# A new order for the last stage of a two-layer network: scores two tiles ahead, the last mix between the upper products, the router shortened

## What is computed

```python
A = softmax((X @ W_q + b_q) @ (X @ W_k + b_k).T / 16); x = layernorm(x + A @ (X @ W_v + b_v))
scores = sigmoid(xf @ gate.T); sfc = scores + corr_bias       # 8 experts in 2 groups of 4
group_scores = top_k(sfc.reshape(N, 2, 4), 2)[0].sum(-1)      # two best of each group
# keep the better group, take its two best experts, normalise their scores
lat = xf @ fc1_w.T
he = relu(lat @ w1[e].T) ** 2 @ w2[e].T                       # for each expert e, weighted and summed
shared = relu(xf @ up_w.T) ** 2 @ down_w.T
x = layernorm(x + comb @ fc2_w.T + shared)
```

## Time and profile before

| | |
|---|---|
| median of three runs | 2061.44 us (2057.5 to 2069.4) |
| the profiled execution | 2061.02 us, of it span 2059.3 us |
| mean granted PE clock over the span | 0.958 of full speed |
| busy over the span | PE 91%, DVE 69%, ACT 42%, POOL 36% |
| one batch of stage C, third of eight | 156.32 us, PE busy 147.09 us |

### The profile page before, as it was taken

How to read it: one execution, slowest core, us unless ns; L and a number is a source line. 1 busy time by engine, 2 the same in 40 slices (tenths; PEclk the granted TensorE clock), 3 DMA queues, 4 the chain that set the end, 5 groups by cost and what they waited for, 6 DMA issues and landing times.

```text
span 2059.3 us, 35698 instructions
## 1 busy us (share of the span) xinstructions
PE 1873.7 (91%) x11728; PEld 1640.9 (80%) x11728; DVE 1413.4 (69%) x3599; ACT 873.6 (42%) x1623; POOL 749.9 (36%) x774
## 2 busy tenths in 40 slices
PE   7999998469999986999999999999999989999997
PEld 6888887359999975878878878878878878878876
DVE  3788787644444446786886886886787787787666
ACT  3445454332322334345445445445445435444433
POOL 4145555431122014244245245145145145144033
PEclk8999999679999997999999999999999999999999
DMA  3111121032222232112112112112112112111011
GB/s 108 62 62 62 62 82 62 22 123 82 92 90 90 81 122 74 32 42 83 42 42 83 37 47 83 37 47 84 34 50 83 32 53 83 32 52 52 11 42 62
DMA packets 80860, 129.94 MB, mean 63 GB/s; under 512 B 11184, under 2 KB 62000, under 8 KB 80720
## 3 DMA queue, kind: packets, MB, share of 16 engines
q1 hardware_dynamic: 71840, 103.91, 15.0%
q0 software_dynamic: 8880, 24.26, 5.0%
HBM read 103.48 MB, written 24.67 MB: 62 GB/s over the span
## 4 chain that ended last, share of the span: by engine, by line
PE 31%; DVE 17%; issue 7%; ACT 4%; POOL 2%; DVEq 0%; DMA 0%; ACTq 0%; POOLq 0%; SPq 0%
PE c_ps L118 6%; PE c_ps L120 6%; PE c_ps L119 6%; PE c_ps L127 3%; PE c_ps L128 3%; PE c_ps L129 3%; PE c_ps L1803 2%; DVE c_shared_place L1720 2%; POOL c_place L1375 2%; DVE c_neg_max L1652 1%; DVE c_tmp L97 1%; DVE c_key L97 1%; DVE c_pre L1562 1%; DVE c_place L1633 1%; DVE c_pre L1560 1%
## 5 line engine op out<-in xcount | busy, mean ns | idle before, releaser
L1375 POOL TENSOR_TENSOR c_place<-c_shared_place,c_place 128x512 fp32r<-128x512 f32 x256 | 329.2, 1310 | 377.2 <-DVE c_shared_place L1720 226.5
L1366 POOL DMA_INDIRECT c_gathered<-expert_results,c_slots x112 | 112.1, 1001 | 361.2 <-DVE c_pre L1562 341.1
L1720 DVE SCALAR_TENSOR_TENSOR c_shared_place<-c_ps,c_shared_place 128x512 f32<-128x512 f32 x256 | 170.3, 683 | 31.7 <-ACT c_shared_place L1505 30.9
L127 PE MATMUL c_ps<-c_downT_hi,c_place 128*128 128x256 f32 x512 | 150.6, 294 | 15.8 <-POOL c_place L1375 15.8
L118 PE MATMUL c_ps<-c_place 128*128 128x256 f32 (+1 forms) x520 | 149.3, 287 | 16.9 <-DVE c_place L1738 9.8
L1513 ACT ACTIVATE c_place<-c_shared_place 128x512 fp32r<-128x512 f32 x128 | 80.3, 630 | 180.8 <-DVE c_shared_place L1720 179.8
L119 PE MATMUL c_ps<-c_place 128*128 128x256 f32 (+1 forms) x520 | 147.9, 284 | 0.0
L120 PE MATMUL c_ps<-c_place 128*128 128x256 f32 (+1 forms) x520 | 147.9, 284 | 0.0
L1462 ACT ACTIVATE c_shared_place<-c_ps,c_shift_s 128x1024 f32<-128x1024 f32 x64 | 71.4, 1116 | 178.5 <-DVE c_shift_s L1656 178.5
L129 PE MATMUL c_ps<-c_downT_hi,c_place 128*128 128x256 f32 x512 | 142.7, 279 | 0.0
L128 PE MATMUL c_ps<-c_downT_lo,c_place 128*128 128x256 f32 x512 | 142.7, 279 | 0.0
(11 more groups left out here) (374 smaller groups left out, 6102.3 us busy)
## 6 DMA issues: line engine op xcount, KB each, us to landing
c_x2T<-score_rows SPq DMA_DIRECT2D x64, 512.0 KB, 5.2
a_xT_raw<-xT SPq DMA_DIRECT2D x8, 1024.0 KB, 6.5
a_x_rows<-x SPq DMA_DIRECT2D x8, 1024.0 KB, 5.6
x_rows<-a_x SPq DMA_DIRECT2D x8, 1024.0 KB, 4.4
c_pre<-x_rows SPq DMA_DIRECT2D x8, 1024.0 KB, 5.5
out<-c_x SPq DMA_DIRECT2D x16, 512.0 KB, 3.0
b_win_raw<-w_in SPq DMA_DIRECT2D x7, 1024.0 KB, 5.5
b_wout_raw<-w_out SPq DMA_DIRECT2D x7, 1024.0 KB, 5.9
```

Of the source, the lines that this page charges most:

```text
L127: pe.matmul(out, lh, rh, start=False, stop=False)
L1366: pool.indirect_dma_start(rows[:, a, :], None, d["ys"], bass.IndirectOffsetOnAxis(ap=slots[:, a, t:t + 1], axis=0), bounds_check=TRASH + P ...
L1375: pool.tensor_tensor(hid_lo[:, place, :], square[:, place % RING, :], f32(hid_hi[:, place, :]), ALU.subtract).then_inc(hid_split, 1)
L1720: v.scalar_tensor_tensor(square[:, place % RING, :], ps[:, s_bank(unit, k - lag), :], 0.0, factor, ALU.max, ALU.mult).then_inc(s_free, 1)
```

## The change

The table is written anew, the buffer `place` is divided anew, the router's group choice has fewer steps, and the down products are taken in another sequence.

```diff
-             ("score", 0), ("v", 2), ("v", 3), ("turn", 0), ("score", 1), ("tail", 0), ("mix", 0), ("combine", 0), ("turn", 1),
+             ("score", 0), ("v", 2), ("v", 3), ("score", 1), ("turn", 0), ("score", 2), ("tail", 0), ("mix", 0),
...
-    ROUTE_STEPS = 2 + 8 + 3 + TOP_STEPS + 5
+    ROUTE_STEPS = 2 + 4 + 3 + TOP_STEPS + 5
...
-        hid_hi, hid_lo = (place[:, 8 * j * SEQ:8 * (j + 1) * SEQ].rearrange("p (k s) -> p k s", s=HALF) for j in range(2))
+        hid_hi, hid_lo = (place[:].rearrange("p (g j k s) -> p j g k s", g=2, j=2, s=HALF)[:, j] for j in range(2))
...
-                chain.then(v.tensor_reduce, marks, groups, AX.X, ALU.max)
-                chain.then(v.tensor_tensor, keys, groups, across(marks, GSIZE), ALU.is_equal)
...
-                chain.then(v.tensor_reduce, seconds, keys1, AX.X, ALU.max)
-                chain.then(v.tensor_tensor, group_m[:], group_m[:], group_n[:], ALU.add)
...
+                chain.then(v.tensor_tensor, larger[:, :, 0:pairs], groups[:, :, 0:pairs], groups[:, :, pairs:GSIZE], ALU.max)
+                chain.step(v.tensor_tensor(sums[:, :, 0:pairs], groups[:, :, 0:pairs], groups[:, :, pairs:GSIZE], ALU.add))
+                chain.then(v.tensor_tensor, sums[:, :, pairs], larger[:, :, 0], larger[:, :, 1], ALU.add)
+                chain.then(v.tensor_reduce, marks, sums[:, :, 0:pairs + 1], AX.X, ALU.max)
...
-                            t, some = 2 * part + k // 2, range(4 * (k % 2), 4 * (k % 2) + 4)
-                            pe.wait_ge(hid_split, hidden(b, "up", (h, k % 2), CHUNKS - 1)[0] + 1)
+                            t, some = 2 * part + k % 2, range(4 * (k // 2), 4 * (k // 2) + 4)
+                            pe.wait_ge(hid_split, hidden(b, "up", (h, k // 2), CHUNKS - 1)[0] + 1)
```

More of the change, by code:

```diff
@@ L1129, in stage_c @@
     ORDER = [("q", 0), ("q", 1), ("q", 2), ("q", 3), ("keep", 0), ("v", 0), ("v", 1), ("keep", 1),
-             ("score", 0), ("v", 2), ("v", 3), ("turn", 0), ("score", 1), ("tail", 0), ("mix", 0), ("combine", 0), ("turn", 1),
[L1131 to L1135, removed]
+             ("score", 0), ("v", 2), ("v", 3), ("score", 1), ("turn", 0), ("score", 2), ("tail", 0), ("mix", 0),
+             ("turn", 1), ("score", 3), ("combine", 0), ("mix", 1), ("combine", 1), ("turn", 2), ("score", 4), ("mix", 2), ("combine", 2),
+             ("turn", 3), ("score", 5), ("combine", 3), ("mix", 3), ("turn", 4), ("ln3", 0), ("score", 6), ("mix", 4), ("norm3", 0),
+             ("turn", 5), ("score", 7), ("combine", 4), ("x3T", 0), ("mix", 5), ("combine", 5), ("turn", 6), ("gate", 0), ("latent", 0),
+             ("gateT", 0), ("mix", 6), ("turn", 7), ("up", (0, 0)), ("scoreT", 0), ("mix", 7), ("ln3", 1), ("up", (0, 1)), ("norm3", 1),
+             ("combine", 6), ("x3T", 1), ("expert", (0, 0)), ("combine", 7), ("ln2", 0), ("gate", 1), ("expert", (0, 1)), ("gateT", 1),
              ("comb", 0), ("up", (1, 0)), ("scoreT", 1), ("out", 0), ("latent", 1), ("up", (1, 1)), ("ln4", 0), ("expert", (1, 0)),
@@ L1614, in route @@
+                chain.then(v.tensor_tensor, choice[:, :, 0:GSIZE], choice[:, :, 0:GSIZE], across(win, GSIZE), ALU.mult)
+                chain.step(v.scalar_tensor_tensor(choice[:, :, GSIZE:EXPERTS], across(win, GSIZE), 0.5, choice[:, :, GSIZE:EXPERTS], ALU.is_lt, ALU.mult))
                 top_two(v, chain, first[:], second[:], choice[:], falling[:], (row_m[:], row_s[:]), row_m[:], (key0[:], key1[:]))
@@ L1863, in body @@
                             pe.wait_ge(hid_split, n + 1)
-                            pe.matmul(out, w2_hi[:, e, :], hid_hi[:, place, :], start=(e == 0), stop=False)
-                            pe.matmul(out, w2_hi[:, e, :], hid_lo[:, place, :], start=False, stop=False)
-                            last = pe.matmul(out, w2_lo[:, e, :], hid_hi[:, place, :], start=False, stop=(e == EXPERTS - 1))
+                            pe.matmul(out, w2_hi[:, e, :], hid_hi[:, place // EXPERTS, place % EXPERTS, :], start=(e == 0), stop=False)
+                            pe.matmul(out, w2_hi[:, e, :], hid_lo[:, place // EXPERTS, place % EXPERTS, :], start=False, stop=False)
+                            last = pe.matmul(out, w2_lo[:, e, :], hid_hi[:, place // EXPERTS, place % EXPERTS, :], start=False, stop=(e == EXPERTS - 1))
                         last.then_inc(v_full, 1)
```

22 lines of the change are left out of this document (8 added, 14 removed).

## The result

The changed kernel takes 2083.25 us (median of five runs, 2078.5 to 2084.3), the kernel before in the same comparison 2068.91. The ratio is 1.0081, with a 95% interval of 1.006 to 1.0103: slower, by 12 to 21 us. My forecast was plus 11 on 2061, so 2072, with 2067 to 2079 as its range; the measured time lies 4 us above that range. Part of the distance is the base: the kernel before took 2068.91 in this comparison and 2061.44 in the three runs that I worked from. On 2061.4 the ratio gives 2078, so the change itself cost 17 us where I had 11. The profiled execution took 2083.25 us, span 2081.5, mean granted clock 0.958, the same as before.

What follows compares the result with a forecast made beforehand. PE was taken as the bound, busy 147.09 of 156.32 us a batch. Terms +2.4 -4.9 +5.4 +1.7 -1.8 -1.0 gave +1.8 a middle batch, 10.9 in all on 2061: 2072, range 2067 to 2079 (chance 0.50).

Steps and rivals of the forecast that it cites:

- Start and middle: From turn 0 to the router: new waits, among them 1.2 and 1.9 ahead of mix 0 and 1; up part 2.4 later.
- Up part and what takes its place: Second up part: wait and low clock go, minus 4.9 us a batch; a new wait ahead of x3T 1, plus 5.4.
- contention term: ln3 1 on DVE beside POOL's subtractions of the first up part: 1.2 us added, ends 0 and 2.2.
- Clock: Low clock behind the new wait at x3T 1: plus 1.7 us a batch, ends 0 and 2.8.
- Down products: Second down products need only the first up part: waits for POOL go, minus 1.8 and minus 1.0 us a batch.
- Last batch: The last batch has no combine (minus 0.3 and minus 1.3), so plus 0.2 us.
- Router: About 1.1 us less on DVE, twice a batch; worth nothing on the path, at most 1.1 if its cover is gone.
- (1): Rival: clock mostly kept behind the new wait or slow stretch hidden; 2061 to 2066, no change; chance 0.22 with (4).
- (2): Rival: faster, norm3 1 not late; gains from a wait of 3.6 down, 2036 at a wait of 2; chance 0.16.
- (3): Rival: DVE stays behind from ln2 on, comb and second half's up wait; plus 3.5 a batch, 2084; chance 0.12.
- (4): Rival: PE's waits merely move by the same amount, the middle of (1); chance 0.22 with (1).

Runs made afterwards that it cites:

- e3: Changed kernel with 18 spare matmuls, results unused, ahead of the wait for x3T 1; ratio 1.0009 to the kernel before.
- e6: Kernel before with the new placement of the squares and new sequence of down products, its own order and router; ratio 0.9921 to the kernel before.
- e5: Kernel before with the shorter router alone; ratio 0.9967 to the kernel before.
- e10: e9 with mix 7 and ln3 1 between the up parts, norm3 1, combine 6 and 7 behind the second; ratio 1.0045 to the kernel before.
- e4: Changed kernel with the first ten units of the mixes in the order of before; ratio 1.0043 to the kernel before.
- e7: Changed kernel with combine 1, 2 and 5 behind the turn and norm3 0 behind turn 5; ratio 1.006 to the kernel before.
- e1: Changed kernel with the four norms (norm3 1) ahead of ACT's work for the second up part; ratio 0.9951 to the kernel before.
- e12: e8 with combine 5 moved from ahead of the router to behind turn 7; ratio 0.9953 to the kernel before.
- e2: Changed kernel with the transposes x3T 1 behind expert (0,0) on every engine; ratio 0.9972 to the kernel before.
- e8: Changed kernel with the changes of e1, e4 and e7 together; ratio 0.9856 to the kernel before.
- e9: Changed kernel with the old ORDER table, keeping new placement, down products and short router; ratio 0.9871 to the kernel before.
- e11: e10 with norm3 1 ahead of the second up part; ratio 0.9949 to the kernel before.

## Why the prediction was right and where it failed

*Start and middle*, plus 2.4 a batch. The first `up` part starts 2.75 later, counted by the work that PE has done up to there (`latent` and mix 7 have changed places with it). The waits are there with their sizes, handover (from the end of one engine's work to the start of the next one's) included: 1.22 for 1.2 ahead of mix 0, 1.87 for 1.9 ahead of mix 1, 0.98 for 0.9, 0.53 and 0.28 for 0.9 at turn 6 and `gate` 0, 1.50 for 1.3. Right.

*Up part and what takes its place.* Up to the start of `x3T` 1 the sum was 2.4 - 4.9 + 5.4 = 2.9, and in the fifth batch before and the fourth after it starts 2.75 later behind `q` 0 (90.92 against 88.17). The wait there is 4.96 with its handover, for 5.4. The missing 0.4 is the contention term, 0.7 smaller than I took it, less some 0.3 of small errors the other way: I took 1.2 for POOL's hit on `ln3` 1, and it was 0.5 (0.70 for 0.17), since POOL started within 0.9 us of DVE's `up` work and was nearly done. That the place of `x3T` 1 came out so close is luck in part: start and middle were 0.35 more than I had, the wait 0.4 less.

*Clock.* The mechanism was right, and the sum failed in the size of two terms, this one and the last batch below. The step here is "For the clock behind it I take 1.7 us, the mean over the eight stretches"; it measured 2.29. Those stretches stand behind waits of 2.6 to 3.3, and one of them, with nothing lost, pulled the mean down. Behind the new wait it costs 1.7 to 1.95 in every other batch and 2.8 in the ones between, 2.29 in the mean and 2.28 by e3, and no batch is spared. The Trainium skill, page "TensorE: Matmul & The Clock Gate", section "HAM oscillation — how this bites in real kernels", says that long pauses between bursts put the array back to half rate each time. For 4.8 us and more the runs agree, in 30 stretches of 30. Behind the shorter waits, 3.3 and 2 us, the clock fell in some batches and not in others. In the same step I booked the 1.5 behind the old wait as a gain. That holds only because the waits for DVE and POOL behind it went too: in the kernel before it cost nothing by itself.

*Down products.* The lead of the changed kernel over its own delay grows by 1.63 at the second down product of the first half and by 1.13 in the second half, 2.76 for my 2.8. Right, though in e6 it is only 1.85, and I had nothing down for what follows: at the first two products of `expert` (1,1) PE now comes a little early for the banks that DVE frees (a wait of 0.08 with its handovers), and 0.4 comes back there. The batch closes: 2.75, plus 1.6 for the clock, less 2.76, plus 0.4, is 2.0 with the clock at 0.70, where such batches are 1.9 longer than before, and 1.2 more with the clock at 0.50. The sum had 1.8.

*Last batch.* This is the second term that failed: I had plus 0.2, by rows of a middle batch. It is plus 3.08. There, before, `combine` 6 and 7 are missing, POOL is earlier and the first of the waits for it is 0.17 instead of 1.65, and the `up` wait 2.56 instead of 3.27. So there was 2.2 less to gain; and the clock behind `x3T` 1 was 0.51. I had taken off what the change adds there less, and not what it gains less: a batch with less work ahead also has shorter waits to remove.

Together: six middle batches 0.7 above my 1.8 (0.6 of it the clock term) and the last 2.9 above, less 0.5 for the first (minus 0.65 for minus 0.1), make 6.6 more than 10.9. That is 17.5 for the last stage, and it agrees with the ratio.

*Router.* "Worth nothing on the path" holds for the new order. What I didn't weigh is that it is an alternative: it takes 1.3 of the 3.27 by itself (e5), and so lowers what moving mix 7 can remove to 2.0. With all else in place the new order costs 6.0 a batch: 4.2 this piece (e10), 1.6 the start (e4), and about 0.6 the middle (e7), which make 6.4 and overlap a little.

*Rivals.* (1) is out, by the windows and e3. (2) gave the point of gain at a wait of 3.6, clock included, and minus 25 us at a wait of 2. e1 has a wait of 1.29 and is 10 us faster than before: the side is right, the size is less than half, since the third down product and `comb` 0 then wait, and the low clock that the old wait brought had cost nothing by itself. (3) didn't come: `comb` 0 has no wait. (4) is the middle of (1).

What stays open: why the clock behind the same wait of 4.81 is 0.65 to 0.70 in every other batch and 0.50 between, and why with a start that is 1.3 us shorter (e4) it fell earlier within the wait. Not tried: `ln3` 1's first step without POOL beside it in the changed kernel's own order.

## What to carry to other kernels

When a move removes a wait, walk on from the moved unit through each engine's queue to its last consumer: here the wait of 3.3 ahead of `up` became 4.8 ahead of `x3T` 1, because two lines of the order put four norms behind squares that weren't urgent. Price a long idle of PE with the clock behind it, from a wait as long as the new one. And where a change has parts that need no new order, run them in the old order first: here these parts alone gave 1.3%, and the new order took that and 0.8% more.

## What the runs showed of the hardware

**Wait and clock.** PE was busy before each of these waits, and the granted clock of the 5.6 us behind them was, over batches 2 to 7: for waits of 4.8 to 5.9 us (the changed kernel, e4, e7, e10, e12) 0.50 to 0.73, in 30 stretches of 30; for 3.25 to 3.28 (before, e6) 0.50 to 0.75 in 11 of 12 and 1.00 in one; for 1.9 to 2.3 (e2, e5, e8, e9, e11) 0.70 or 0.72 in 18 and 1.00 in 12; for 1.29 (e1) 1.00 in six of six. With the wait filled by matmuls (e3) it was 1.00 in six of six. Taking every wait of 1.2 to 1.87 us in these batches of all runs: behind those of 1.70 to 1.87 it was 0.70 in 5 stretches of 36 (mix 1 in e1, e2 and e7, the down product in two batches of e5) and 1.00 in the rest, and behind those of 1.2 to 1.69 it was 1.00 in 98 of 98. So a wait of 2 us can be followed by 1.7 us of lost clock or by none.

**A small DVE instruction beside POOL.** L142 has two inputs of 128x4 in SBUF and takes 0.17 us alone. In three cases where it started while POOL's four subtractions (1.26 us each) ran, it ended within 0.03 us of POOL's last one: 1361.32 and 1361.29 in the changed kernel, 1343.03 and 1343.00 in e8, 1347.07 and 1347.04 in e12, so that it took 0.70, 1.17 and 3.09. In the first two it started within the last subtraction. In e12 it started within the second and stayed through the two behind it. But in the earlier trace rows it ended at 1245.77, when one subtraction ended and POOL's group had 1.2 us to go. So it ended with a subtraction each time, and how many it is held through isn't settled by these runs. The Trainium skill, page "GPSIMD Engine Reference", section "1. Specifications", says that the two engines share their SBUF interfaces and that DVE instructions with two SBUF inputs contend. The runs agree, though not for every such instruction. Two steps of a `combine` read `gathered` and `pre`, both in SBUF, beside one group of the changed kernel (timelines of DVE and POOL):

```profile
1367.50 0.47 DVE L1560 SCALAR_TENSOR_TENSOR c_pre<-c_gathered,c_gates,c_pre 128x256 f32<-128x256 f32 x1
1368.01 1.37 DVE L1562 SCALAR_TENSOR_TENSOR c_pre<-c_gathered,c_gates,c_pre 128x256 f32<-128x256 f32 x1
...
1365.10 5.40 POOL L1375 TENSOR_TENSOR c_place<-c_shared_place,c_place 128x512 fp32r<-128x512 f32 x4 [3.81 <-DVE c_shared_place L1716]
```

The first took its usual 0.47, the second 0.9 more. DVE instructions that read PSUM ran on beside the same kind of subtractions at their usual 0.69 (the row at 1358.01 above).
